# Macaron block with a Mamba-2 scan: when GpSimd does its first eight sums, and where VectorE makes S in step 13

## The reference, cut to what matters

```python
# x: 1 x 2048 tokens x 512 channels, float32
x = x + 0.5 * ffn(layernorm(x))            # 4-bit dequantised weight + LoRA + bias
x = x + block(layernorm(x))                # below
x = x + 0.5 * ffn(layernorm(x))

def block(x):
    h = x + mamba2(rmsnorm(x, ln1_w))      # 4 heads, state 128, causal conv of 4 taps, chunks of 128 tokens
    h2 = rmsnorm(h, ln2_w)
    return h + (silu(h2 @ gate.T) * (h2 @ up.T)) @ down.T      # inner width 1792

# in mamba2, for chunk c and each head (cs: running sum of dt*A in the chunk):
#   att   = (C B^T) * exp(cs_q - cs_k) * dt        masked to k <= q
#   Y     = att @ X + C @ state_before * exp(cs) + D * X
#   state = exp(cs_end) * state_before + (weights * B)^T @ X
```

## Time and profile before

| | before |
|---|---|
| median of 3 runs | 766.13 us |
| the profiled execution's own time | 765.96 us |
| its span, first to last instruction | 764.1 us |
| PE busy | 752.9 us (99%), 3418 matmuls |
| DVE busy | 629.2 us (82%), 1237 instructions |
| ACT busy | 446.5 us (58%) |
| POOL busy | 338.0 us (44%), 392 instructions |
| granted TensorE clock | 1.0 throughout |

### The profile page before, as it was taken

One profiled execution on the slowest core, in us unless ns is written; L12 is line 12 of the kernel. 1 busy time (PEld: TensorE's weight loads), 2 busy tenths in 40 slices (PEclk: granted clock), 3 DMA queues, 4 the chain that ended last, 5 costly groups with the idle time before them and its releaser, 6 DMA issues.

```text
span 764.1 us, 10562 instructions
## 1 busy us (share of the span) xinstructions
PE 752.9 (99%) x3418; PEld 352.2 (46%) x3418; DVE 629.2 (82%) x1237; ACT 446.5 (58%) x881; POOL 338.0 (44%) x392
## 2 busy tenths in 40 slices
PE   8999999999999999999999999999999999999998
PEld 3444544454554444444444444444444444444444
DVE  7798878878878979878799978878878878767994
ACT  4867867677786675644545556456456456444441
POOL 5631544663442379775414233243243233224574
PEclk9999999999999999999999999999999999999999
DMA  8933544543331122420421733733733743443564
GB/s 300 196 76 71 144 87 86 110 98 70 69 70 26 30 42 54 98 56 1 118 49 27 179 70 70 164 70 69 164 72 68 163 74 64 78 80 69 111 178 138
DMA packets 95558, 71.86 MB, mean 94 GB/s; under 512 B 65248, under 2 KB 72672, under 8 KB 95504
## 3 DMA queue, kind: packets, MB, share of 16 engines
q0 software_dynamic: 17280, 31.46, 23.0%
q1 hardware_dynamic: 77744, 39.66, 19.9%
q10 hardware_dynamic: 480, 0.07, 0.1%
HBM read 20.32 MB, written 4.19 MB: 32 GB/s over the span
## 4 chain that ended last, share of the span: by engine, by line
PE 67%; DVE 18%; ACT 6%; issue 4%; DMA 2%; POOL 1%; ACTq 0%; SPq 0%; DVEq 0%; POOLq 0%
PE PS L1990 61%; DVE raw L1468 3%; PE PS L2115 2%; DVE state L1450 2%; PE PS L2123 1%; DVE stage L1468 1%; DVE st L1303 1%; DMA x_t<-hb 1%; DVE S L1433 1%; DVE xs L1400 1%; ACT xds L845 1%; ACT pre L895 1%; ACT raw L896 1%; DVE x L1459 1%; DVE w_in L1573 1%
## 5 line engine op out<-in xcount | busy, mean ns | idle before, releaser
L723 POOL DMA_DIRECT2D xs<-x x59 | 51.0, 864 | 153.4 <-ACT x L1170 139.6
L1990 PE MATMUL PS<-h,w_in 128*128 128x512 f16 x480 | 108.7, 379 | 0.7 <-DMA h<-hn_p 0.7
L1990 PE MATMUL PS<-h,x_t 128*128 128x512 f16 x408 | 94.0, 379 | 0.0
L1990 PEld LDWEIGHTS PS<-h,w_in 128*128 128x128 f16 x480 | 46.9, 98 | 65.8 <-issue 15.7
L1990 PE MATMUL PS<-n_T,stage 128*128 128x512 f16 x288 | 71.5, 379 | 0.0
L1170 ACT ACTIVATE x<-PS,d_d 128x512 f32<-128x512 f32 x59 | 40.2, 682 | 39.7 <-PE PS L1990 38.7
L1990 PEld LDWEIGHTS PS<-h,x_t 128*128 128x128 f16 x408 | 39.5, 98 | 48.5 <-issue 2.3
L529 POOL TENSOR_TENSOR r<-mv,mhalf 128x1 f32<-128x1 f32 (+1 forms) x32 | 29.4, 920 | 67.5 <-DVE mv L1307 53.1
L723 POOL DMA_DIRECT2D xs<-n x29 | 25.2, 869 | 67.7 <-ACT n L1170 58.3
L1990 PE MATMUL PS<-pre,stage 128*128 128x512 f16 x192 | 49.3, 379 | 0.0
L1140 ACT ACTIVATE xds<-tm,dgh 128x512 f32<-128x512 f32 x24 | 17.3, 722 | 52.7 <-DVE tm L1914 52.7
(11 more groups left out here) (320 smaller groups left out, 1823.1 us busy)
## 6 DMA issues: line engine op xcount, KB each, us to landing
xs<-x POOLq DMA_DIRECT2D x75, 256.0 KB, 3.3
xs<-n POOLq DMA_DIRECT2D x29, 256.0 KB, 3.3
x_t<-x_in SPq DMA_DIRECT2D x16, 256.0 KB, 3.0
x_t<-hb POOLq DMA_DIRECT2D x16, 256.0 KB, 3.9
out<-x_t SPq DMA_DIRECT2D x15, 256.0 KB, 2.3
raw_gu<-gate_t SPq DMA_DIRECT2D x7, 512.0 KB, 4.5
raw_gu<-up_t SPq DMA_DIRECT2D x7, 512.0 KB, 6.5
raw_d<-down_t SPq DMA_DIRECT2D x7, 512.0 KB, 7.5
```

What stands on the lines that cost most here:

```text
L723: po.dma_start(chunk_of(xs, c), d_tmps[d % 3], accum_op=ALU.add).then_inc(s_acc[d % 3], 16)
L1990: ins = pe.matmul(out_, lhs(a, b, k), rhs(a, b, k), start=first and n == 0, stop=last and n == len(todo) - 1)
```

## The change

Sums 0 to 7 move to steps 8, 9, 10 and 11, two in each, all behind `rms2` of the step. `scan_c(12)` goes back to its ordinary place, at the start of step 11. In step 13 VectorE calls `weights(14)` and `scan1(14)` ahead of `advance(13)` instead of behind it. No instruction is added or removed.

```diff
@@ GpSimd, step(c)
                 if c + 1 < NCH:
-                    if c != 2 * CH + 3:
-                        scan_c(c + 1, (c + 1) % CH)
+                    scan_c(c + 1, (c + 1) % CH)
                     scan_d(c + 1, (c + 1) % CH)
...
                 rms2(c, c % CH)
-                if c == 2 * CH + 2:
-                    scan_c(c + 2, (c + 2) % CH)
                 if not early_sums:
                     sums(c)
...
-            T_EARLY = {2 * CH + 2: range(0, 3), 2 * CH + 3: range(3, 8), 3 * CH: range(8, 12),
+            T_EARLY = {2 * CH: range(0, 2), 2 * CH + 1: range(2, 4), 2 * CH + 2: range(4, 6), 2 * CH + 3: range(6, 8),
+                       3 * CH: range(8, 12),
                        3 * CH + 1: range(12, 16), 3 * CH + 2: range(16, 20)}
@@ VectorE, step(c)
-                advance(c, j)
+                if c != 3 * CH + 1:
+                    advance(c, j)
                 if c + 1 < NCH:
                     weights(c + 1, (c + 1) % CH)
                     scan1(c + 1, (c + 1) % CH)
+                if c == 3 * CH + 1:
+                    advance(c, j)
```

## The result

The changed kernel takes 767.81 us (median of 7 runs, 767.32 to 770.93), the kernel before 765.77 (7 runs, 764.95 to 766.16; the first three of them gave the 766.13 above). The ratio is 1.0034, 95% interval 1.0020 to 1.0047: slower, by 2.0 us in the medians. (The ratio is made over all the runs; that of the two medians is 1.0027.) Two executions of 1502 us (the kernel before) and 1612 us (e6) are left out of all ratios. The profiled execution's span is 765.6 us, against 764.1.

A forecast was written before the change was run, and what follows sets the result against it. DVE was taken to bound steps 8 to 13, with PE close behind. Sums add 4.5 us in steps 8 and 9, steps 12 to 14 give back 2.9: +1.6 on 765.96, so 767.5 us, range 763.2 to 769.3.

The forecast's parts named there:

- The bound: Steps 8 to 13: DVE is the bound with PE close behind; PE takes over at 308.47 us.
- Step 8: Sums 0 and 1 behind rms2 each hold a DVE instruction; PE is 2.1 us later at chunk 10.
- Step 9: Sums 2, 3 and scan_c(11) hold DVE 2.4 us more; PE waits 1.3 to 1.4 at L2044, rest at L2080.
- rival C: POOL keeps the port over two instructions without a wait between; one or two holds of 1.2 us more, 768.8 to 769.5; chance 0.07.
- Together 4.5: Cost added in steps 8 and 9, 2.1 + 2.4 us, with bounds 3.1 and 5.1.
- Chunk 12: PE's wait before chunk 12, 0.67 us: 0.5 taken as gained, bounds 0 and 0.67.
- Chunk 13: With fewer sums POOL is idle when S comes, so PE's wait of 1.16 us goes whole.
- Chunk 14: S with its diagonal comes 2.3 us earlier, 1.0 from the swap; PE can use 1.26.
- The sum: Whole kernel: +4.5 us in steps 8 and 9, -2.9 in steps 12 to 14, so +1.6 us, 767.5 us.
- Rival A: Sums in steps 8 and 9 are free in POOL's idle time; only the gain stays, 762.9 us; chance 0.22.
- B: Half the hold falls on PSUM-reading DVE instructions or idle time; 2.2 to 3 us added, 765.3 to 766.1; chance 0.17.
- D: The swap in step 13 fails, advance(13) late for L2097; at most 1.1 us on top, 768.6; chance 0.04.

The follow-up runs named there:

- e6: Kernel before plus eight GpSimd memsets, four behind rms2 of step 8 and four behind that of step 9; 765.39 us, ratio 0.9999.
- e4: Kernel before with only sums 0 and 1 moved, from step 10 to step 8; 767.83 us, ratio 1.0034.
- e5: Kernel before with only sums 0 and 1 moved, from step 10 to step 9; 767.82 us, ratio 1.0030.
- e9: Kernel before plus swap, sums 6 and 7 behind chunk 13's mask, T4's cast and low part later in step 12; 765.70 us, ratio 1.0001.
- e2: Changed kernel with the swap of step 13 taken back, so the sums' schedule alone; 768.45 us, ratio 1.0041.
- e8: Changed kernel plus extra TensorE matmuls filling its two long gaps, 8 before chunk 10's S wait, 6 before csm(3); 769.07 us, ratio 1.0043.
- e7: Kernel before plus four extra sums, two behind rms2 of step 8 and two of step 9, real sums unmoved; 769.97 us, ratio 1.0058.
- e10: As e9, but only sum 7 goes to step 12, sum 6 stays in step 11; 765.49 us, ratio 0.9997.
- e1: Kernel before with only the swap in step 13 (advance(13) behind weights(14) and scan1(14)); 765.14 us, ratio 0.9999.
- e11: Changed kernel with the sums of steps 8 and 9 ahead of rms2 instead of behind it; 764.74 us, ratio 0.9990.
- e12: As e11, with sums 2 and 3 also moved into step 8, none in step 9; 765.84 us, ratio 1.0003.

## Why the prediction was right, point by point

**The bound.** Right. DVE sets the pace of steps 8 to 13. e4 and e5 show it from one side (two sums beside DVE there cost 2.4 us), e9 from the other (a wait of PE taken away comes back, with S of chunk 14 ready at the same time).

**Step 8: +2.1 us forecast.** Measured 2.36 (e4: 2.35). The order was otherwise: the tap at 236.83 did not go first and hold sum 0, but was held itself; from there on as described, one instruction for each sum, and `scan_c(10)` a third.

**Step 9: +2.4.** Undersized. DVE's L1627 ran at 264.16 against 259.54: 4.62, plus 0.45 because this execution is that much ahead at chunk 9, less the 2.36 of step 8, is 2.7 us. The sum came earlier, too, than the prediction had it: 0.68 us behind the DMA's start and not 0.90, and so beside the first tap and not the second. That tap of 3.47 us spans sums 2 and 3, as rival C had it for instructions without a wait between them (C named other pairs). In e5, where the two sums have a wait between them, the same count gives 2.4 us. The consumers were named rightly: L2044's wait is 1.54 us (1.3 to 1.4 forecast), the rest was to show at L2080, and does in e2 and e8 (0.83 instead of 0.49).

**Together 4.5.** e7 measures it alone: 5.4 us, above the upper bound of 5.1, or 5.05 by e2, where the clock stayed up, just below it (2.35 + 2.35, and 0.35 more at L2080). The bound counted full lengths of the four sums and not what they do to `scan_c` behind them.

**Chunk 12: -0.5.** In e2 and e8 the interval from 11 to 12 is 0.3 us shorter than before. It holds the longer wait at L2080, which belongs to step 9; against e7, which has that wait as well, it is 14.31 - 13.63 = 0.68 us shorter. So the wait before chunk 12 went whole, the upper bound of 0.67.

**Chunk 13: -1.16.** 1.25, as a number right. As a gain it was misread: taken alone (e9, e10 against e1) nine tenths or more of it come back in the next interval. Here it counted because DVE, too, came earlier in step 13: S of chunk 14 at 306.15 instead of 304.80 where S of chunk 13 is at 291.48 instead of 287.62, so 2.5 us regained, near the 2.3 forecast; L1538's hold is gone (1.27 us).

But the 1.0 that the forecast put down to the swap is not in these 2.5. In e2, without the swap, the same stretch is as short (306.90 - 292.24 = 14.66 us, against 14.67), for what the swap saves `weights(14)` loses (1.44 us instead of 0.41). What e2 regains is 0.9 at L1538, 0.6 at `weights(14)` (0.41 instead of 1.01) and 1.0 that the forecast didn't have: the two instructions of L1527 take 1.62 us together instead of 2.64. That the number fits is in part luck.

**Chunk 14: -1.26.** PE waited for nothing there, 12.53 us. That isn't owed to its being late from the slow matmuls: e11, with the clock up, has 12.54. In e8 it is 13.21, with no wait for S either, but one of 0.51 us for the gating, behind the held `lo2`. So the whole 1.26 is gained where `lo2` goes first, and 0.7 where it doesn't; the prediction did not see that this would hang on 0.05 us. The swap's part is 13.57 - 13.21 = 0.36 us (e2 against e8), and 0.43 in e1, not 1.03, for it sent `weights(14)` into `scan_c(14)`.

**The sum, +1.6, 767.5 us.** Measured 2.0 in the medians, 767.81. In the traces it is 2.14 us. Errors in opposite directions did not quite meet: some 0.55 too little added (5.05 against 4.5; 0.9 if e7's 5.4 is taken), some 0.4 too little given back (3.3 us, 0.67 + 1.25 + 1.36, where 2.9 were forecast), and the clock, which the sum left out, with about 0.4. That a mechanism right in the main gives a number 0.3 us off owes something to luck. **Rival A** is refuted by e4, e5 and e7, **B** by the same (its 2.2 to 3 us are what the sums cost in another place: 2.37 + 0.35 in e11), **D** by e1. The swap did fail to bring S earlier, though, because of `weights(14)` and not, as D had it, because of the state. **C** was true as a mechanism in step 9, at 0.3 us instead of 1.2; two of its holds would have made 770.0 us, not 769.5.

## What to carry to other kernels

Idle time of GpSimd is no free place if VectorE is the bound there: ask first which VectorE instructions stand beside it, and whether they have two SBUF inputs. A wait of TensorE that goes away is a gain only if the engine it waited for is not the bound itself; read the chain of waits for the last one that binds. And another place a few us away can halve such a cost (e11 against e2: the same four sums, 2.4 us instead of 4.7), and 0.05 us between two engines can decide over 0.7 (`lo2` and `scan_c(13)`), so such placements have to be tried, not only reasoned. When two kernels are compared to price one thing, look first whether such a meeting fell the same way in both traces (e8 against the change).

## What the runs showed of the hardware

A VectorE instruction whose recorded start came first did not always go first. In the changed kernel the tap starts at 236.83 us and sum 0 at 237.12, both beside the accumulating DMA of POOL (236.44, 0.90 us), and the tap ends at 239.09, 0.56 us behind the sum's end at 238.53: as if held from its start, for its usual 0.75 us end at 239.09 only if they begin at 238.34. The DMA alone doesn't do it: before the change a tap came 0.38 us behind such a DMA and took 0.75, and so it is with a memset behind it (e6). Here the Trainium skill's rule for who blocks whom (same page and section: issue order decides) and the trace differ; going by recorded starts, the sum that follows the DMA wins although it comes 0.3 us later. It was so each time that a sum stood there beside a tap (e2, e4, e5, e7 and e8 too). And it isn't only behind a DMA: in e2, e8 and e12 `scan_c(13)` wins over the `lo2` that started 0.05 us ahead of it, in the change and e11 it waits. At starts 0.10 to 0.28 us apart with no DMA just ahead, as before the change at 241.00 (a tap) and 241.11 us (`scan_c(10)`), DVE, which started first, went first.

Over two sums without a wait between them POOL kept going, with the tap held for both (3.47 us), while with a semaphore between them (sums 0 and 1) DVE got in between. e5 has these two sums in the very place of step 9, behind the same DMA, and there the tap takes 2.26 us; so it is not the place that makes the difference, but the wait or the kind of sum. It isn't a rule either: before the change `scan_c(13)` follows sum 7 without a wait (290.09 us), and DVE's L1573 got in between, as the 1.72 us of `scan_c(13)` show.

The two gaps of 2.48 and 1.54 us on TensorE, 12 us apart, were followed by a granted clock of 0.80 over 6 us and 24 matmuls in 7.04 us instead of 5.34; in e8 gaps of 0.74 and 0.24 us left it at 1.00. In e2, with gaps of 2.46 and 1.54 us, it stayed at 1.00 too, so such gaps allow the drop but don't force it. Nor is the second gap needed: in e7 the clock fell right behind the first, of 2.47 us (0.79 over 250 to 256 us).
